# A four-part graph network on one core: one attention stage in groups of three tiles instead of four

## What is computed

```python
def _agnn_layer(h, src, dst, beta, num_nodes):
    h_norm = h * jax.lax.rsqrt(jnp.sum(h * h, axis=-1, keepdims=True) + EPS)
    cos = jnp.sum(h_norm[src] * h_norm[dst], axis=-1)
    logits = beta * cos
    m = jax.ops.segment_max(logits, dst, num_segments=num_nodes)
    ex = jnp.exp(logits - m[dst])
    denom = jax.ops.segment_sum(ex, dst, num_segments=num_nodes)
    alpha = ex / (denom[dst] + EPS)
    msg = alpha[:, None] * h[src]
    return jax.ops.segment_sum(msg, dst, num_segments=num_nodes)
```

## Time and profile before

| | us |
|---|---|
| median of 2 runs (8363.69 to 8364.05) | 8363.87 |
| the profiled execution, its own time | 8360.1 |
| its span from first to last instruction | 8358.4 |

### The profile page before, as it was taken

How to read it: one execution, slowest core, us unless ns; L and a number is a source line. 1 busy time by engine, 2 the same in 40 slices (tenths; PEclk the granted TensorE clock), 3 DMA queues, 4 the chain that set the end, 5 groups by cost and what they waited for, 6 DMA issues and landing times. The chain is left out here.

```text
span 8358.4 us, 152930 instructions
## 1 busy us (share of the span) xinstructions
PE 5760.2 (69%) x32873; PEld 4634.0 (55%) x33057; DVE 5311.7 (64%) x15276; ACT 3000.4 (36%) x7465; POOL 5337.3 (64%) x5324
## 2 busy tenths in 40 slices
PE   0004445535556966997997997998588878887886
PEld 0004435534445845776776776777366656665664
DVE  8003347664441237777777777777688868887888
ACT  0001100000011214444444444444466646655664
POOL 4777777757712136776776776776377657756774
PEclk9996677766678978999999999999799989999998
DMA  6001123323308953333343333433233333323332
GB/s 231 10 2 46 53 67 103 103 79 105 105 29 278 371 183 94 106 105 102 105 106 102 105 105 102 106 105 90 74 94 95 87 82 94 94 71 96 95 93 72
DMA packets 597887, 866.00 MB, mean 104 GB/s; under 512 B 273775, under 2 KB 412013, under 8 KB 596374
## 3 DMA queue, kind: packets, MB, share of 16 engines
q0 software_dynamic: 233280, 595.84, 25.5%
q1 hardware_dynamic: 364502, 269.16, 10.6%
HBM read 740.80 MB, written 125.75 MB: 104 GB/s over the span
## 5 line engine op out<-in xcount | busy, mean ns | idle before, releaser
L1760 POOL DMA_INDIRECT hs<-tab_agnn,rec x1952 | 1896.7, 972 | 649.5 <-issue 557.4
L2203 POOL DMA_INDIRECT hs<-tab_gat,rec x1464 | 1602.6, 1095 | 577.3 <-issue 432.3
L1826 DVE CUSTOM_DVE_ANT_0 prod<-psG,hs 128x256 f32<-128x256 f32 x1952 | 829.3, 480 | 408.8 <-DMA hs<-tab_agnn,rec 320.8
L1889 PE MATMUL psG<-HN,ohT 128*128 x3904 | 965.3, 391 | 14.8 <-DVE lg L1826 7.9
L2235 DVE TENSOR_REDUCE mt<-psL 128x2 f32<-128x1024 f32 x732 | 860.1, 1216 | 144.9 <-PE psL L2356 87.6
L1906 PE MATMUL psV<-hs,pr 128*128 128x258 f32 x3904 | 931.5, 382 | 0.0
L1843 ACT ACTIVATE prT<-cand,mn 128x512 f32<-128x512 f32 x488 | 352.3, 722 | 1166.6 <-DVE mn L1786 1159.6
L1889 PEld LDWEIGHTS psG<-HN,ohT 128*128 128x128 f32 x3904 | 710.0, 192 | 108.3 <-issue 19.7
L1906 PEld LDWEIGHTS psV<-hs,pr 128*128 128x128 f32 x3904 | 706.1, 191 | 80.1
L2372 PE MATMUL psV<-msg,oh 128*128 128x260 f32 x2928 | 732.7, 395 | 0.0
L805 PE MATMUL psT<-ident,oh 128*128 128x128 f32 x416 | 95.9, 373 | 857.5 <-DVE oh L770 857.5
(11 more groups left out here) (340 smaller groups left out, 12092.3 us busy)
## 6 DMA issues: line engine op xcount, KB each, us to landing
w<-in_L_gnn_w SPq DMA_DIRECT2D x224, 512.0 KB, 5.8
hs<-tab_agnn,rec POOLq DMA_INDIRECT x1952
fwd_d<-acc SPq DMA_DIRECT2D x10, 2730.0 KB, 34.1
fw<-fwd_d SPq DMA_DIRECT2D x104, 260.0 KB, 2.7
hs<-tab_gat,rec POOLq DMA_INDIRECT x1464
rec<-rec_d SPq DMA_DIRECT2D x1166, 10.0 KB, 1.8
b<-in_L_gnn_b SPq DMA_DIRECT2D x113, 128.0 KB, 6.4
x<-xbuf SPq DMA_DIRECT2D x112, 128.0 KB, 6.0
```

What stands on the lines that cost most here:

```text
L1760: nc.gpsimd.indirect_dma_start(out=hs[:, j, g, :], out_offset=None, in_=k.tab_agnn, in_offset=bass.IndirectOffsetOnAxis(ap=rec[:, j, g, 0: ...
L1826: ins = V.tensor_tensor_reduce(prod[:, h2, g, :], psG[:, bank(j2, half), m, :], hs[:, j2, g, 0:D], hs[:, j2, g, D:D + 1], 0.0, ALU.mult, A ...
L1889: mm = nc.tensor.matmul(psG[:, bank(j1, half), m, :], ohT[:, j1 % 2, 2 * half + m, :], pick(HN, b, slice(None)).rearrange("p a c -> p (a c ...
L2203: nc.gpsimd.indirect_dma_start(out=hs[:, j, g, :], out_offset=None, in_=k.tab_gat, in_offset=bass.IndirectOffsetOnAxis(ap=rec[:, j, g, 0:1 ...
```

## The change

Angle attention takes the tiles in groups of `GA = 3`; graph attention and the message stages stay at four. The constant number of groups becomes `NGA = 155`, so a layer issues 465 gathers where it issued 488. All tiles of that stage that were four wide are three wide (`cand`, `oh`, `psL` and so on have 384 columns and not 512). Since the groups begin at other tiles, they need their own table, `gb3`: DVE computes it behind `place_edges`, SP carries it through HBM, and DVE copies both tables into `gbr` and `gbr3` (32 small copies), so POOL has no copies behind the scatter. The wait counts of the semaphores that run through all stages are recomputed (`landed` and others).

```diff
+GA = 3
+NGA = (E + NB * (GA * P - 1)) // (GA * P)
...
-        prod = sb("prod", [P, 2, J], F32)
+        prod = blk
...
+        def groups_of_three(dve):
+            V = nc.vector
+            c = Chain(dve, s_gb3)
+            V.memset(gb3, 0)
...
             def _(dve):
                 place_edges(dve)
+                threes = groups_of_three(dve)
+                assert threes == THREES
                 dve.wait_ge(k.sems.x, 32)
                 norm.on_vector(dve)
+                dve.wait_ge(s_gbd, 112)
+                dve.wait_ge(s_gb3d, 16 * (2 * COLS_A + 2))
+                for to, of, turns in ((k.gbr, k.gb, TURNS), (k.gbr3, gb3, TURNS_A)):
+                    rowv = to[:, :, :].rearrange("o n (i c) -> o n i c", c=ROW)
+                    for c in range(ROW):
+                        lo = 2 * U - ROW_AT + c
+                        nc.vector.tensor_copy(rowv[:, :, :, c], of[:, :, lo:lo + turns * U].rearrange(
+                            "o n (i s) -> o n i s", s=U)[:, :, :, 0])
...
+                sp.wait_ge(s_gb3, THREES)
+                for n in range(2):
+                    for c in range(COLS_A):
+                        sp.dma_start(k.gb3_d[n, c * P:(c + 1) * P, :], gb3_i[:, c, n:n + 1]).then_inc(s_gb3d, 16)
+                sp.wait_ge(s_gb3d, 16 * 2 * COLS_A)
+                for n in range(2):
+                    sp.dma_start(gb3[:, n, 2 * U:2 * U + COLS_A * P], k.gb3_d[n, :, :].rearrange("g k -> k g")).then_inc(s_gb3d, 16)
+                sp.wait_ge(s_gb3d, 16 * (2 * COLS_A + 2))
...
-                pool.wait_ge(s_gbd, 112)
-                rowv = k.gbr[:, :, :].rearrange("o n (i c) -> o n i c", c=ROW)
-                for c in range(ROW):
-                    lo = 2 * U - ROW_AT + c
-                    nc.gpsimd.tensor_copy(rowv[:, :, :, c], k.gb[:, :, lo:lo + TURNS * U].rearrange(
-                        "o n (i s) -> o n i s", s=U)[:, :, :, 0])
...
-        rec = sb("rec", [P, U, G, 5], I32)
-        hs = sb("hs", [P, U, G, W_AGNN])
...
+        rec = sb("rec", [P, U, GA, 5], I32)
+        hs = sb("hs", [P, U, GA, W_AGNN])
...
-                nth = lambda t: layer * NG + (2 * NE + t)
...
+                nth = lambda t: layer * NGA + (2 * NE + t)
+                use = lambda i, j: layer * uses(j, NGA) + (2 * uses(j, NE) + i)
+                landed = lambda i, j: layer * (uses(j, NGA) * (16 * GA)) + (2 * uses(j, NE) * (16 * G) + i * (16 * GA))
...
-                        for g in range(G):
-                            if g == G // 2:
-                                if back := lagged(i, j, 1):
+                        for g in range(GA):
+                            if g == GA // 2:
+                                if back := behind(i, j, 1):
                                     i_, j_, _ = back
-                                    pool.wait_ge(q.gather[j_], use(i_, j_) * (16 * G) + 16 * G)
+                                    pool.wait_ge(q.gather[j_], landed(i_ + 1, j_))
                                     pool.sem_inc(q.gate_pool, 1)
...
-                                for m in range(2):
+                                for m in range(min(2, GA - 2 * half)):
```

More of the change, by code:

```diff
@@ L1731, in _ @@
                     state_on_sync(sp)
-                    starts = RowNumbers(nc, sp, turn_rows(k, 1), "start", T)
+                    starts = RowNumbers(nc, sp, turn_rows(k.gbr3, 1), "start", T)
                     def step(i, j):
@@ L1736, in step @@
                         if not (isinstance(i, int) and i == 0):
-                            sp.wait_ge(q.gather[j], use(i, j) * (16 * G))
+                            sp.wait_ge(q.gather[j], landed(i, j))
                             sp.sem_inc(q.gate_sp, 1)
@@ L1770, in _ @@
                     state_on_vector(dve)
-                    blocks = RowNumbers(nc, dve, turn_rows(k, 0), "block", lag=7)
+                    blocks = RowNumbers(nc, dve, turn_rows(k.gbr3, 0), "block", lag=7)
                     def step(i, j):
-                        now, mid_, old, add = (lagged(i, j, n) for n in (0, 2, 4, 7))
+                        now, mid_, old, add = (behind(i, j, n) for n in (0, 2, 4, 7))
                         if old:
@@ L1817, in step @@
                             h2 = j2 % 2
-                            dve.wait_ge(q.gather[j2], use(i2, j2) * (16 * G) + 16 * G)
+                            dve.wait_ge(q.gather[j2], landed(i2 + 1, j2))
                             if not (isinstance(t2, int) and t2 < 2):
@@ L1835, in step @@
                     def step(i, j):
-                        last, old, done = (lagged(i, j, n) for n in (1, 4, 5))
+                        last, old, done = (behind(i, j, n) for n in (1, 4, 5))
                         if old:
@@ L1868, in _ @@
                     pe.sem_inc(q.gate_pe, 1)
-                    blocks = RowNumbers(nc, pe, turn_rows(k, 0), "block", lag=1)
+                    blocks = RowNumbers(nc, pe, turn_rows(k.gbr3, 0), "block", lag=1)
                     def step(i, j):
-                        now, last, cos, old, add = (lagged(i, j, n) for n in (0, 1, 2, 3, 5))
+                        now, last, cos, old, add = (behind(i, j, n) for n in (0, 1, 2, 3, 5))
                         if now:
@@ L1913, in step @@
                                 pe.wait_ge(s_p, own(t3))
[L1914 removed]
+                            for g in range(GA):
                                 mm = nc.tensor.transpose(psP[:, g * P:(g + 1) * P], prT[:, j3 % 2, g * P:(g + 1) * P], k.ident[:, :])
                             mm.then_inc(s_turn, 1)
[L1917 removed]
+                    pipeline(pe, step, 5, NGA, numbers=blocks)
         s_x = sem("s_x")
@@ L2176, in _ @@
                     def _(sp):
-                        starts = RowNumbers(nc, sp, turn_rows(k, 1), "start", T)
+                        starts = RowNumbers(nc, sp, turn_rows(k.gbr, 1), "start", T)
                         def step(i, j):
```

114 lines of the change are left out of this document (76 added, 38 removed).

## The result

| | kernel before | changed kernel |
|---|---|---|
| median of its runs | 8363.87 us | 8854.8 us (8851.99 and 8857.6) |
| profiled execution | 8360.1 us | 8851.99 us |
| its span | 8358.4 us | 8850.3 us |
| mean granted clock of TensorE | 0.892 | 0.875 |

The change makes the kernel slower: ratio 1.0588, 95% interval 1.0569 to 1.0606. The forecast was 8864 us. By the profiled executions it is +491.9 us where +500 was forecast.

A forecast was written before the change was run, and what follows sets the result against it. POOL's stream of gathers was taken as the bound, with a landing wait stalling every group of three: 510 - 8 - 2 = +500 us on 8360.1, so 8860, and 8864 us with the runs' median 3.8 us higher; range 8760 to 8950.

The forecast's parts named there:

- What bounds the kernel: Angle attention: POOL issues gathers back to back, one every 1.287 us, four to a group, 5.14 us a group.
- hidden today by 0.19 us: Landing wait before the third of four gathers: landing plus release takes 3.56 us, POOL gets there after 3.75 us.
- The stall of 1.06 us in every group: Second of three gathers in angle attention: POOL would arrive after 2.50 us but may not start before 3.56.
- 4.88 us a group of three: Angle attention's period: landing 2.79, release 0.77, third gather 1.25 later, plus 0.07; 510 us more in four layers.
- the term of 0.07 us: Part of the group period: what two gathers take longer than 1.25 us, 0.037 us each.
- The end of a layer, -8: After an angle layer's last gather, steps a quarter narrower in part save 2 us a layer, 8 in all.
- The new table, -2: Beside the scatter: DVE's table work is hidden and POOL's 16 copies leave the path, saving 2 us.
- Graph attention: nothing: Graph attention keeps its groups, waits and counts, so no change in time, unchanged to a few us.
- The start of the kernel unchanged to a few us: Sign to look for in the changed kernel's trace: the kernel's start unchanged to a few us.
- The second, a falling clock: Rival: TensorE's clock falls in angle attention, PE bounds part of the groups, 155 us more, about 9020; chance 0.05.
- The third: Rival: gathers land in 2.3 us with fewer in flight, period 4.32 us, kernel 8520 us; chance 0.04.
- its first rival: No stall in angle attention, POOL back to back, 465 gathers at 1.287 us, kernel 8237 us; chance 0.06.

## Why the prediction was right

**What bounds the kernel.** "POOL's stream of gathers sets the length of a layer", "hidden today by 0.19 us": right. Taking the wait further back changed nothing (0.9997), moving it one gather forward cost 592 us.

**The stall of 1.06 us in every group.** Right in mechanism and size. The landing was 2.79 us, as taken; the release 0.75 us, where 0.77 was; the idle time before the second gather mostly 1.3 to 1.4 us, where 1.4 was; in 582 groups of 620 it ended by a landing, 787.6 us in all where 840 was forecast. POOL also waited for `psV`, 38 times and 49.7 us in all, ahead of a group's first gather; where it did, the landing had mostly come before the second gather's turn.

**"4.88 us a group of three."** 4.87 measured, so 504 us where 510 was forecast. That it came so near is in part luck, for the term of 0.07 us, 43 us of the 510, had a reason that didn't hold. Gathers didn't take longer than the bare pitch (mean 950 ns, 972); and with a median of 4.79 us the usual period is the bare loop, 2.79 + 0.75 + 1.25. The mean is 0.08 us higher by some 60 groups, and by two things that the prediction doesn't name. The waits for `psV` delay a first gather so far that the second starts 1.0 to 1.3 us behind the landing; that is 18 us in all, and most of it went, and the kernel got 11 us quicker, when PE was kept busy. And sixteen times, four times a layer, POOL stood for 1.9 us (twice for 1.4) ahead of a third gather, which is 25 us more than its usual 0.30:

```profile
3375.61 0.94 POOL L1819 DMA_INDIRECT hs<-tab_agnn,rec  x1 [1.93 <-issue]
```

They come 33 groups apart, at the same four groups of every layer, and also with PE kept busy. In the kernel before POOL never stood for over 0.32 us ahead of a third or fourth gather. Nothing in the profile ends them, and their cause is open.

**The end of a layer, -8.** About -13 came (the 5.9 us of the three gaps and the 7.1 us behind the last layer). After a layer's last gather PE is now through in 11.5 us, where it was 14.2:

```profile
3944.46 0.94 POOL L1819 DMA_INDIRECT hs<-tab_agnn,rec  x1 [0.31 <-issue]
...
3953.18 2.78 PE L1965 MATMUL psV<-hs,pr 128*128 128x258 f32 x12
```

which is 2.7 us for the 2 taken; the rest of the 13 has no row of its own that I read.

**The new table, -2.** Wrong in sign. The step itself is right: POOL's 16 copies went from the path, and the next stage's first load comes 2.4 us earlier. But by itself, in groups of four, the table costs 12 us (8374.74), in stages whose instructions it leaves as they were. The sum hid it: the terms for the table and the ends were forecast at -10 together, and everything outside the layers came out at -12 in the changed kernel. That the two numbers are near is luck.

**"Graph attention: nothing"**: 709.8, 709.4 and 710.0 us a layer for 707.8, within the few microseconds said. "The start of the kernel unchanged to a few us": the angle stage starts 3.1 us later, but in it the backward stage is 8.6 us longer (554.1 for 545.4).

**The rivals.** The second, a falling clock, was refuted for this kernel: 11 us, not 155. But of what was said in the trace's terms two numbers were off: the clock was 0.95, not near 1.00, and PE was busy for 83%, not 72%. The clock explains little of the second: from 3340 to 3380 us it was 1.00, and PE was busy for 84% (the numbers behind the stretch are its length and PE's busy time),

```profile
3340.00:3380.00 40.00, 33.47 (x184) 25.41 (x182) 25.20 (x107) 16.14 (x40) 22.73 (x25) 1.00 0.32 82
```

so PE's busy time in a group, taken at three quarters of what it was, fell by less than that, from 4.68 to 4.05 us (581.48 / 700 x 4.87). The third was refuted by the landing: 2.79 us with fewer transfers in flight (DMA share 0.32), as before. The Trainium skill's formula (DMA: Bandwidth & Descriptors, Anatomy of one DMA), about 2.0 us and the bytes over 436 GB/s, gives an estimate of 2.3 us for these 133 KB. The rows of the changed kernel don't agree: they have 2.79 once more, and they decide.

**Where the prediction failed is the price of its first rival.** It said: "If POOL's stall were gone, its 3 x 1.287 = 3.86 us would be next", and 8237 us. With the wait hidden the kernel took 8567. Busy times per group were summed there, and the once-a-turn pauses left out: 1.7 us on DVE and on PE and the clock behind them, and perhaps a ring of buffers that holds a quarter less. That bound lies at 4.43 us a group. It didn't touch the forecast, since 4.88 is above it, but it would have misled anyone who hid the wait next.

So of the 491 us between the medians, 287 go when the landing wait is hidden. 12 are the table's, taken alone. The other 192 are what separates groups of three with a hidden wait (8567) from groups of four with the same table (8375); the clock behind the pauses accounts for some 80 of these, as shown; that the pauses themselves and the shorter ring do the rest was argued, not tried by itself.

## What to carry to other kernels

A wait ahead of the n-th transfer of a group has only the transfers before it to hide behind; when groups get smaller, compare the flight time plus the release (here 2.79 + 0.75 us) with the transfers left (here 2.50 us) before anything else. Before pricing the case in which a stall is removed, look for what happens once a loop turn, not only at busy time per group: groups that are a quarter smaller make such costs a third more frequent per tile. And a change that touches only small instructions elsewhere can move a kernel by half a per cent in stages that it leaves alone, so a gain of a few microseconds is to be measured, not summed.

## What the runs showed of the hardware

- From the pass of the landing wait to the start of the gather behind it took 0.75 to 0.76 us in 579 of 616 groups of the changed kernel, with POOL standing for 0.6 to 2.6 us before the gather. In the other 37, whose first gather was late, it took 1.0 to 1.3 us.
- In groups of four with the early wait the last gather of a group took 1.2 to 1.4 us on average in four of the six places in the turn, where it took 0.95 us in the other two and most other gathers did everywhere. Why it stretches no run shows.
- A pause of 1.7 us of PE, once in some 27 us in which it was otherwise busy for over four fifths, was followed by a fall of the granted clock (0.72 over 6 us) in 69 turns of 103, with another gap of 1.4 us some microseconds ahead of it; five-fold transposes just ahead of the pause kept it at 1.00. In the kernel before, with pauses of 1.4 to 1.5 us once in some 31 us and PE busy for 91%, it was 1.00.
- 16 small copies moved from POOL to DVE, more than 5 ms earlier, made graph attention 10 to 12 us a layer slower (three layers, 707.8 to between 718.0 and 720.0); with the second table made as well it was slower by 0.6 to 1.3 us. The cause is open.
